# Routing, value placing and residual moved between VectorE, ScalarE, TensorE and GpSimd in an eight-part transformer kernel

## The chip, the cores and the metric

The kernel runs on one core of one Trainium2 chip. The metric is the device time of one execution, in microseconds; times below count from the start of the profiled span. The engines are TensorE (PE; PEld is its weight load), VectorE (DVE), ScalarE (ACT), GpSimd (POOL) and SyncE (SP). They run side by side, each in the order of its own list, and wait for each other on semaphores.

## The reference

Sixty-four batches of 128 tokens with 128 features go through four layers, each a cross attention and a feed-forward part, each added to its input after a layer norm. The change touches the last layer, and at its end the output:

```python
x = x + _L3_xattn_ref(_layernorm(x), ctx, ctx, Uq, Vq, bq, ... Uo, Vo, bo)
x = x + _L3_ffn_ref(_layernorm(x), router_w, w1, w2)
```

The attention of layer 3 has 16 heads of 8 features, 77 keys a batch, projections of the form `x U V + b`, and keeps the 64 largest of the 77 scores before its softmax. Its feed-forward part is a mixture of 64 experts: every token goes to the four experts with the largest router probability (position within an expert by token order, 128 places an expert), each expert computes `silu(h1) * h2` and a second product, and a token's result is the sum of its four experts' rows weighted by their probabilities.

## The kernel before, in words

All eight parts are one program. `X` (128 x 64 x 128) stays in SBUF for its whole length. `attention_layer` (from L128) writes all four attention parts; for layer 3 it is called with `topk=64`, `lowrank=True`, a context and a router. It first opens a short block: SP loads the weights (`load`, L233), the products `U V` are folded into `Wq, Wk, Wv, Wo` on TensorE (L298) and copied (L290), and `router.load` (L2426) and `router.prepare` (L2431) add what the router needs.

The main block has one list of steps for each engine, written out by `run_written_out`: step s works on several batches at once. For layer 3 (`lag = 2`) TensorE computes in step s the scores of batch s, turns the scores of batch s-2, weighs the values of s-2, turns back s-3, projects the output of s-4 (`project_out`, L439), and prepares s+1. ScalarE evacuates PSUM: `copy_scores` (L565) copies raw scores, first and second half, `probabilities` (L538, L540) makes exponentials, `copy_q` (L548) and `spread_k` (L554) fill the operands of the next scores. VectorE does the selection of the 64 largest: for each of 16 heads eight smallest distances are found (`select_eight`, L727), replaced (L735), found again (L743) and replaced (L756); between them stand `residual` (L783, adds the projected output in PSUM to `X`), `subtract_max` (L696), `norm_heads` (L676, L681), `place_v` (L774, puts the projected values with their bias into `vaug`) and `statistics` (L788). GpSimd computes `distances` (L630) and adds the output bias to `X` (`add_bias`, L618).

The router rides on the same steps, four batches (a group, 16 in all) at a time, four steps a group: on GpSimd `deviations`, `probabilities` (L2594), `chosen` (L2601, L2608: the mask of chosen experts and running counts), `place` (L2613 to L2629: the row of each token in its expert's table), `fill_rows` (L2635 to L2637) and `scatter` (L2645), 16 indirect DMAs a group that send the token rows to DRAM. On VectorE stand `minima` (L2685), `sums` (L2689), `reciprocals`, `best` (L2701), `marks` (L2715) and `keys_in_order` (L2725); on ScalarE and TensorE normalisation, logits, and positions (`copy_positions`, L2515). Group g is handled from step 4g+8 on, so its last steps lie up to 14 steps behind the last attention batch: a tail in which the routing runs alone.

Then a small block loads `own` and `rank` and clears `hid` (L2824 to L2829), the expert block runs 32 pairs of experts and sends their rows on to a table of shares, and the last block adds up: for each batch SP loads the four shares of every token (L3003, 256 KB), TensorE adds in PSUM the product of the last expert rows (L3013) and `X` through an identity product (L3015), VectorE adds the shares pairwise (L3023, L3035) and then PSUM (L3031), and ScalarE's queue stores 64 KB. Four buffers stand behind each of these tiles.

Of the kernel before, what the change touches and what calls it, by code (L numbers as in the profile page):

```python
# [127 lines left out]
def attention_layer(nc, m, k, w, heads, keys, scale, context=None, mask=None, topk=0, lowrank=False,  # L128
# [28 lines left out]
    with ExitStack() as ctx:  # L157
# [30 lines left out]
        if lowrank:  # L188
            U = sb("U", [D, 4, D])
            V = sb("V", [D, 4, D])  # L190
# [17 lines left out]
        v_ps = PS[0:keys, 7, 128:256]  # L208
# [18 lines left out]
        with nc.Block() as block:  # L227
# [3 lines left out]
            def _(sp):  # L231
# [30 lines left out]
            def _(dve):  # L262
# [24 lines left out]
                if lowrank:  # L287
                    dve.wait_ge(q["fold"], 1)
                    for n, W in enumerate((Wq, Wk, Wv, Wo)):
                        last = dve.tensor_copy(W[:, :], PS[:, 0, n * D:(n + 1) * D])  # L290
                    last.then_inc(q["prep"], 1)

            @block.tensor
            def _(pe):
                if lowrank:
# [4 lines left out]
                    last.then_inc(q["fold"], 1)  # L300
            m.weight_loads = loaded
# [26 lines left out]
        def _(pe):  # L328
# [21 lines left out]
            def project_context(i, u, h):  # L350
# [3 lines left out]
                else:  # L354
                    pe.wait_ge(q["xT"], q.nth("xT", i))
                    kv = yT
                if past(i, 1):
                    pe.wait_ge(q["v"], q.nth("v", i, 1))
                    if not topk:
                        pe.wait_ge(q[k_ready], q.nth(k_ready, i, 1))  # L360
# [4 lines left out]
                if not topk:  # L365
                    pe.matmul(kT_ps, Wk[:, :], kv[:, u, :], start=True, stop=True)
# [64 lines left out]
            def project_out(i, u):  # L431
# [3 lines left out]
                pe.wait_ge(q["v"], q.nth("v", i, -(lag + 2)))  # L435
                if router is not None:
                    router.tensor_projected(pe, i + lag + 2)
                if inner is None:
# [50 lines left out]
        def _(act):  # L489
# [67 lines left out]

            def copy_scores(i, u, half):
# [14 lines left out]
            def step(s, v, h):  # L573
# [32 lines left out]
            run_written_out(act, step, 2 if y_by_scalar else 1, max(lag + 1, beyond), slots=slots)  # L606
# [60 lines left out]
        def _(dve):  # L667
# [124 lines left out]
            def step(s, v, h):  # L792
                u, a = v % 2, (v + 1) % 2
                end, fin = s - lag - 1, s - lag - 2
                if topk:
# [3 lines left out]
                    if real(fin):  # L799
                        residual(fin, (v - lag - 2) % 2)  # L800
# [10 lines left out]
                    if real(s + 1):  # L811
                        place_v(s + 1, (v + 1) % slots)
# [1557 lines left out]
def make_router(nc, m, t, ctx, wfT, row):  # L2370
# [41 lines left out]

    def have(i):
# [8 lines left out]
    def load(sp):  # L2422
        loads = [(gate[:, :], t[n + "router_w"]), (before_f[:, :], t["c_before"]),
                 (slot0[:, :], t["c_slot0"]), (code[:, :], t["c_token"])]
# [5 lines left out]
    def prepare(dve):  # L2430
        dve.memset(ones[:, :], 1.0)  # L2431
# [159 lines left out]
    def probabilities(pool, i):  # L2591
        prob = rows_of(i)[:, :, D:D + E]
        pool.wait_ge(q["rec"], i + 1)
        pool.tensor_tensor(prob, prob, bcast(rec[:, :], 2, E), ALU.mult).then_inc(q["prob"], 1)  # L2594

    def chosen(pool, i):
        u = i % 2
        pool.wait_ge(q["marked"], i + 1)
        if i >= 1:
            pool.wait_ge(q["pos"], i)  # L2600
        pool.tensor_scalar(by_expert(mask[:, u, :]), mark[:, :].rearrange("p (g e) -> p g e", e=E + PAD)[:, :, 0:E], -1.5,  # L2601
                           None, ALU.is_lt).then_inc(q["mask"], 1)
        pool.wait_ge(q["mask"], i + 1)
        for g in range(G):
            if g or i:
                pool.wait_ge(q["ahead"], G * i + g)
            out = ahead[:, u, g + 1, :] if g < G - 1 else ahead[:, (u + 1) % 2, 0, :]
            pool.tensor_tensor(out, ahead[:, u, g, :], mask[:, u, g * E:(g + 1) * E], ALU.add).then_inc(q["ahead"], 1)  # L2608

    def place(pool, i):  # L2610
        u = i % 2
        pool.wait_ge(q["posc"], i + 1)
        pool.tensor_scalar(near[:, :], posc[:, :], CAP - 1.0, None, ALU.min).then_inc(q["near"], 1)  # L2613
        pool.tensor_scalar(over[:, :], posc[:, :], float(CAP), float(SLOTS), ALU.is_ge, ALU.mult).then_inc(q["over"], 1)
        pool.wait_ge(q["near"], i + 1)
        pool.tensor_tensor(by_expert(key[:, :]), by_expert(near[:, :]), bcast(slot0[:, :], 1, G), ALU.add) \
            .then_inc(q["key"], 1)
        pool.wait_ge(q["over"], i + 1)
        pool.tensor_tensor(far[:, :], over[:, :], mask[:, u, :], ALU.mult).then_inc(q["far"], 1)
        pool.wait_ge(q["key"], i + 1)  # L2620
        pool.tensor_tensor(near[:, :], key[:, :], mask[:, u, :], ALU.mult).then_inc(q["kept"], 1)
        if i >= 1:
            pool.wait_ge(q["skeytop"], i)
        pool.wait_ge(q["far"], i + 1)
        pool.wait_ge(q["kept"], i + 1)
        pool.tensor_tensor(skey[:, :], near[:, :], far[:, :], ALU.add).then_inc(q["skey"], 1)
        if i >= 1:
            pool.wait_ge(q["wfTps"], i)
        pool.tensor_tensor(by_expert(wf[:, :]), by_expert(far[:, :]), rows_of(i)[:, :, D:D + E], ALU.mult) \  # L2629
            .then_inc(q["wf"], 1)  # L2630

    def fill_rows(pool, i):
        pool.wait_ge(q["skeytop"], i + 1)
        s3 = skeytop[:, :].rearrange("p (g e) -> p g e", e=8)[:, :, 0:K]
        pool.tensor_copy(rows_of(i)[:, :, KEYS:KEYS + K], s3)  # L2635
        pool.tensor_copy(rows_of(i)[:, :, CODE:CODE + 1], code[:, G * i:G * i + G].unsqueeze(2))
# [600 lines left out]
```

## Time and profile before

| | |
|---|---|
| median of three runs | 3944.61 us (3942.61 to 3950.3) |
| the profiled execution's own time | 3949.06 us |
| its span | 3947.3 us |
| mean granted TensorE clock | 0.837 |
| busy: TensorE, VectorE, ScalarE, GpSimd | 76%, 76%, 57%, 48% |
| attention of layer 3 (2702 to 3634 us) | 932 us |
| routing tail (3634 to 3742 us) | 108 us |
| last block (3850.5 to 3947.3 us) | 96.8 us |

The page gives for each engine its busy time as a share of the span, and its digits cut the span into 40 slices of 98.7 us. TensorE's two clock levels are 1.2 and 2.4 GHz; a granted clock of 0.50 is the lower one. In a timeline row the first number is the start, the second the duration; xN merges neighbours of one line. The shares are averages over stages with different limits, so they are read by stage.

### The profile page before, as it was taken

What the parts mean: (1) busy time and instruction counts of PE and PEld (TensorE: products, weight loads), DVE (VectorE), ACT (ScalarE), POOL (GpSimd) and SP (SyncE); (2) the same over time, 40 slices, a digit from 0 to 9 for tenths busy, and PEclk for the clock granted to TensorE, in tenths of its full rate; (3) what the DMA queues carried; (4) which work ended last, traced back from release to release, by engine and by line L of the source; (5) the groups of instructions that cost most, each with busy time, mean ns of one, the idle gap of its engine ahead of it and who ended that gap; (6) DMA issues with size and microseconds to landing.
All of it is one profiled execution on the core that took longest, in us unless ns stands there. A gap on an engine that the chain in (4) does not pass through costs nothing. (4 is left out here: it accounts for less than half of the span.)

```text
span 3947.3 us, 77991 instructions
## 1 busy us (share of the span) xinstructions
PE 3004.5 (76%) x23435; PEld 1888.8 (48%) x23435; DVE 3014.5 (76%) x12267; ACT 2240.8 (57%) x4368; POOL 1905.5 (48%) x2166
## 2 busy tenths in 40 slices
PE   3777776999979997797599968885777767777069
PEld 1222222444447776443467745554555555555046
DVE  6999997666667776344788858887999999998065
ACT  4999997333346665242366646664666666665030
POOL 5777776000014566575444442222256666666660
PEclk9999998999989999898799979996555665655585
DMA  2000000940000010253200000000011100000037
GB/s 74 5 5 5 5 6 22 418 193 0 0 16 17 27 29 26 79 140 111 61 15 15 15 8 2 2 2 13 20 36 38 38 18 5 5 5 2 1 111 213
DMA packets 161015, 177.77 MB, mean 45 GB/s; under 512 B 71762, under 2 KB 136180, under 8 KB 153179
## 3 DMA queue, kind: packets, MB, share of 16 engines
q1 hardware_dynamic: 127964, 140.65, 11.7%
q0 software_dynamic: 23424, 27.94, 2.1%
q10 hardware_dynamic: 9216, 4.20, 0.4%
q8 instruction: 197, 3.23, 0.3%
q14 instruction: 214, 1.75, 0.1%
HBM read 80.48 MB, written 113.61 MB: 49 GB/s over the span
## 5 line engine op out<-in xcount | busy, mean ns | idle before, releaser
L395 PE MATMUL PS<-IDENT,a_T 128*77 128x128 f32 (+1 forms) x3584 | 618.3, 313 | 132.0 <-ACT a_Pr L540 110.5
L1037 ACT ACTIVATE l_H<-l_H 128x2048 f32<-128x2048 f32 (+2 forms) x256 | 597.3, 2702 | 2.8 <-POOL l_H L1089 2.6
L395 PEld LDWEIGHTS PS<-IDENT,a_T 128*77 128x77 f32 (+1 forms) x3584 | 487.0, 171 | 226.8 <-ACT a_Pr L540 88.6
L1089 POOL TENSOR_TENSOR l_H<-l_feat,l_text 128x4096 f32<-128x4096 f32 x64 | 450.4, 7039 | 131.5 <-PE PS L993 130.8
L993 PE MATMUL PS<-l_H,l_wide 128*32 128x512 f32 (+1 forms) x2560 | 332.2, 595 | 165.3 <-ACT l_H L1037 165.3
L1111 DVE TENSOR_TENSOR l_H<-PS,l_text 128x2048 f32<-128x2048 f32 (+1 forms) x192 | 411.7, 2146 | 2.1 <-ACT l_text L1064 2.1
L542 ACT ACTIVATE a_Pr<-PS 77x512 f32<-77x512 f32 (+1 forms) x640 | 375.4, 588 | 59.4 <-PE PS L395 59.4
L412 PE MATMUL PS<-a_Pr,a_vaug 77*32 77x128 f32 (+1 forms) x7168 | 303.9, 316 | 21.8 <-ACT a_OT L571 15.8
L630 POOL TENSOR_TENSOR a_T<-a_mx,a_T 128x616 f32<-128x616 f32 x128 | 155.5, 1215 | 307.4 <-DVE a_mx L696 307.4
L2645 POOL DMA_INDIRECT expert_rows<-e3r_row,e3r_rows_at x256 | 253.6, 991 | 86.7 <-issue 73.6
L109 POOL TENSOR_TENSOR RSTD<-norm_tmp,MINUS_HALF 128x24 f32<-128x24 f32 x6 | 25.1, 4189 | 553.3 <-DVE norm_tmp L102 553.3
L338 PE MATMUL PS<-a_kblk,a_qT 32*128 32x308 f32 (+1 forms) x2048 | 243.1, 549 | 24.2 <-ACT e3r_posc L2515 7.4
L637 POOL TENSOR_TENSOR a_T<-a_T,a_mx 128x616 f32<-128x616 f32 x128 | 155.6, 1216 | 204.0 <-DVE a_mx L712 204.0
L412 PEld LDWEIGHTS PS<-a_Pr,a_vaug 77*32 77x32 f32 (+1 forms) x7168 | 214.1, 125 | 76.2 <-issue 54.2
L528 ACT ACTIVATE a_yT<-PS 128x128 f32<-128x128 f32 x192 | 53.3, 278 | 301.1 <-PE PS L348 301.1
L993 PEld LDWEIGHTS PS<-l_H,l_wide 128*32 128x32 f32 x2560 | 57.5, 109 | 342.7 <-ACT l_H L1037 294.6
L735 DVE MATCH_REPLACE8 a_T<-a_r,a_T 128x77 f32<-128x77 f32 x1024 | 213.6, 222 | 0.3 <-issue 0.3
L756 DVE MATCH_REPLACE8 a_T<-a_r,a_T 128x77 f32<-128x77 f32 x1024 | 213.6, 223 | 0.0
L429 PE MATMUL PS<-IDENT,a_O 128*128 128x128 f32 x256 | 86.1, 336 | 160.0 <-DVE a_O L681 160.0
L714 DVE TENSOR_REDUCE a_mx<-PS 128x8 f32<-128x616 f32 (+1 forms) x256 | 189.2, 739 | 22.9 <-PE PS L338 13.7
L1492 ACT ACTIVATE e_act_g<-PS 128x512 f32<-128x512 f32 x128 | 76.5, 597 | 225.8 <-PE PS L1444 225.6
L716 DVE TENSOR_TENSOR a_T<-PS,a_mx 128x616 f32<-128x616 f32 (+1 forms) x256 | 190.8, 745 | 8.8
(356 smaller groups left out, 7857.7 us busy)
## 6 DMA issues: line engine op xcount, KB each, us to landing
pair_rows<-e_zero SPq DMA_DIRECT2D x35, 1024.0 KB, 25.3
expert_shares<-e_zero SPq DMA_DIRECT2D x16, 1024.0 KB, 25.7
e3c_four<-expert_shares SPq DMA_DIRECT2D x64, 256.0 KB, 3.2
e_xin<-pair_rows SPq DMA_DIRECT2D x39, 264.0 KB, 3.2
e_four<-pair_shares SPq DMA_DIRECT2D x16, 512.0 KB, 4.5
e_w<-in_L_ffn_blocks SPq DMA_DIRECT2D x39, 194.0 KB
e3x_xin<-expert_rows SPq DMA_DIRECT2D x32, 200.0 KB
expert_rows<-e_zero SPq DMA_DIRECT2D x6, 1024.0 KB, 24.8
```

What stands on the lines that cost most here:

```text
L338: last = pe.matmul(PS[:, g, 0:hpg * keys], qT[32 * g:32 * g + 32, u, :], kblk[32 * g:32 * g + 32, u, :], start=True, stop=True, tile_posit ...
L395: last = pe.transpose(PS[0:keys, 4 + g % 2, j * S:(j + 1) * S], T[:, u, c:c + keys], m.IDENT[:, :])
L412: last = pe.matmul(PS[32 * j:32 * j + 32, 6, g * S:(g + 1) * S], vaug[:, v, c * 32:c * 32 + 32], Pr[:, u, c * S:(c + 1) * S], start=(p == ...
L542: act.activation(part, turned, ACT.Exp).then_inc(q[f"P{g}"], 1)
L716: dve.tensor_tensor(t4, raw, bcast(m4, 3, keys), ALU.subtract).then_inc(q[f"sfree{half}"], 1)
L735: last = dve.match_replace(t3[:, h, :], r1[:, u, 8 * h:8 * h + 8], t3[:, h, :], FAR)
L756: last = dve.match_replace(t3[:, h, :], r2[:, u, 8 * h:8 * h + 8], t3[:, h, :], FAR)
L993: last = pe.matmul(PS[32 * j:32 * j + 32, 4 + u, 0:cols], wide[:, 32 - r:64 - r], H[:, u, CH * c * S:CH * c * S + cols], start=(r == 0), s ...
L1037: act.activation(cells, cells, ACT.Tanh).then_inc(q[f"tanh{part}"], 1)
L1089: pool.tensor_tensor(H[:, a, lo * S:hi * S].rearrange("p (t f) -> p t f", f=S), bcast(feat[:, a, :], 1, hi - lo), bcast(text[:, a, lo:hi], ...
L1111: dve.tensor_tensor(H[:, u, lo * S:hi * S].rearrange("p (t f) -> p t f", f=S), bcast(PS[:, 1 + u, 0:S], 1, hi - lo), bcast(text[:, u, lo:h ...
L2645: pool.indirect_dma_start(out=m.rows[:, :], out_offset=bass.IndirectOffsetOnAxis(ap=rows_at[:, i % 3, g * K + k:g * K + k + 1], axis=0), i ...
```

## The change

- **Values.** `place_v` of VectorE is replaced by `place_v_plain` on ScalarE, a copy of the projected values from PSUM without their bias. The bias of the values is instead carried through the output projection once, in the setup: `bv` as a column is widened to a 128 x 128 tile, multiplied by `Wo`, and added to `bo`. The projected values move from bank 7 to bank 4 and are computed together with keys and queries.
- **Residual.** In `project_out` an identity product adds `X` (with the output bias already in it) in PSUM, and ScalarE writes the sum to `X` (`write_x`). `residual` leaves VectorE's list for this layer.
- **Late routing.** `probabilities` of group 15, `chosen` of groups 14 and 15, `place` and `fill_rows` of groups 13 to 15 are issued by VectorE instead of GpSimd.
- **Setup of the experts.** `own`, `rank` and `hid` are loaded and cleared in the attention layer's setup; the block of their own goes.
- **Last block.** For odd batches TensorE's identity product goes; VectorE adds `X` to the half sum, waits for that, and goes on.

```diff
@@ setup of the lowrank layer @@
+                if lowrank:
+                    load(bv_col[:, :], w.bv.unsqueeze(1))
...
-                    last.then_inc(q["prep"], 1)
+                    dve.tensor_copy(bv_wide[:, :], bv_col[:, 0:1].broadcast_to([D, S])).then_inc(q["prep"], 1)
+                    dve.wait_ge(q["fold"], 2)
+                    dve.tensor_tensor(bo[:, :], bo[:, :], PS[:, 1, 0:D], ALU.add)
...
+                    pe.wait_ge(q["prep"], m.preps + 3)
+                    pe.matmul(PS[:, 1, 0:D], bv_wide[:, :], Wo[:, :], start=True, stop=True).then_inc(q["fold"], 1)
@@ TensorE @@
                 if topk:
                     pe.matmul(kT_ps, Wk[:, :], cT[:, u, :], start=True, stop=True)
+                    pe.matmul(v_ps, cT[:, u, :], Wv[:, :], start=True, stop=True)
...
+                        pe.wait_ge(q["v"], q.nth("v", i, -lag))
...
+                if topk:
+                    if past(i, 1):
+                        pe.wait_ge(q["x"], q.nth("x", i, 1))
+                    pe.matmul(out_ps, OT[:, u, :], Wo[:, :], start=True, stop=False)
+                    pe.wait_ge(q["bias"], q.nth("bias", i))
+                    last = pe.matmul(out_ps, m.IDENT[:, :], seq(m.X, i), start=False, stop=True)
@@ ScalarE @@
+            def place_v_plain(i, v):
+                if past(i, slots):
+                    act.wait_ge(q["pv"], q.nth("pv", i, slots))
+                act.activation(head_columns(vaug[:, v, :], hps)[:, :, :, 0:dh],
+                               v_ps.rearrange("p (t a e) -> p t a e", a=hps, e=dh), ACT.Copy).then_inc(q["v"], 1)
+
+            def write_x(i):
+                act.wait_ge(q["out"], q.nth("out", i))
+                act.activation(seq(m.X, i), out_ps, ACT.Copy).then_inc(q["x"], 1)
...
                     probabilities(use, (v - lag) % 2, 0)
+                if topk and real(use - 2):
+                    write_x(use - 2)
...
                         spread_k(s + 1, a)
+                        place_v_plain(s + 1, (v + 1) % slots)
@@ VectorE @@
-                    if real(fin):
-                        residual(fin, (v - lag - 2) % 2)
...
-                    if real(s + 1):
-                        place_v(s + 1, (v + 1) % slots)
@@ router @@
+    late_weighed, late_chosen, late_placed = NG - 1, NG - 2, NG - 3
...
+        if v == 0 and have(c - 3) and c - 3 >= late_weighed:
+            probabilities(dve, c - 3)
+        if v == 2 and have(c - 3) and c - 3 >= late_placed:
+            place(dve, c - 3)
...
+        if v == 0 and have(c - 3) and c - 3 >= late_chosen:
+            chosen(dve, c - 3)
+        if v == 2 and have(c - 3) and c - 3 >= late_placed:
+            fill_rows(dve, c - 3)
@@ last block @@
-                    pe.matmul(PS[:, s % 4, 0:D], m.IDENT[:, :], m.X[:, s, :], start=False, stop=True) \
-                        .then_inc(q["far"], 1)
+                    if s % 2 == 0:
+                        last = pe.matmul(PS[:, s % 4, 0:D], m.IDENT[:, :], m.X[:, s, :], start=False, stop=True)
+                    last.then_inc(q["far"], 1)
...
+                        if w % 2:
+                            dve.tensor_tensor(two[:, w, 0:D], two[:, w, 0:D], m.X[:, s - 1, :], ALU.add) \
+                                .then_inc(withx, 1)
+                            dve.wait_ge(withx, (s - 1) // 2 + 1)
```

## Rows read from the trace of the kernel before

**Rows 1.** Windows by stage: window, length, each engine's busy us, PEclk, DMA share, GB/s.

```profile
2702.00:3634.00 932.00, 675.55 (x4672) 496.27 (x4672) 911.18 (x6892) 592.13 (x1376) 538.26 (x770) 0.58 0.06 18
3634.00:3742.00 108.00, 19.10 (x129) 14.40 (x128) 12.32 (x86) 13.08 (x33) 82.74 (x114) 0.50 0.02 1
3850.50:3947.30 96.80, 92.69 (x256) 63.87 (x256) 52.92 (x192) 0.00 (x0) 0.00 (x0) 0.50 0.76 217
```

**Rows 2.** Timeline of VectorE from L727 to what follows: start, us, line, operation.

```profile
2727.55 0.22 DVE L727 MAX8 a_r<-a_T 128x8 f32<-128x77 f32 x1
2727.91 0.09 DVE L735 MATCH_VALUE_LOAD a_T<-a_r,a_T 128x8 f32 x1
...
2766.38 2.33 DVE L727 MAX8 a_r<-a_T 128x8 f32<-128x77 f32 x16
2768.62 0.27 DVE L783 TENSOR_TENSOR X<-PS,X 128x128 f32<-128x128 f32 x1
2768.85 0.09 DVE L735 MATCH_VALUE_LOAD a_T<-a_r,a_T 128x8 f32 x1
...
3260.55 0.27 DVE L783 TENSOR_TENSOR X<-PS,X 128x128 f32<-128x128 f32 x1
3260.74 0.41 DVE L2685 TENSOR_REDUCE e3r_mn<-e3r_nl 128x4 f32<-128x256 f32 x1
```

**Rows 3.** Timeline of VectorE at L774.

```profile
3267.83 0.27 DVE L774 TENSOR_TENSOR a_vaug<-PS,a_bv 77x128 f32<-77x128 f32 x1
3268.01 0.41 DVE L2689 TENSOR_REDUCE e3r_lsum<-e3r_row 128x4 f32<-128x256 f32 x1
```

**Rows 4.** Timelines of TensorE, ScalarE, VectorE in the step with least margin.

```profile
3243.60 1.41 PE L338 MATMUL PS<-a_kblk,a_qT 32*128 32x308 f32 x8 [0.53 <-ACT e3r_posc L2515]
...
3247.89 0.66 ACT L565 ACTIVATE a_T<-PS 128x616 f32<-128x616 f32 x1
...
3249.68 0.78 DVE L696 TENSOR_REDUCE a_mx<-a_T 128x8 f32<-128x616 f32 x1
```

**Rows 5.** Timeline of the setup block, SP's last issues.

```profile
2696.30 0.43 SPq L2426 DMA_DIRECT2D e3r_slot<-in_c_slot  x1
2696.77 0.43 SPq L2426 DMA_DIRECT2D e3r_code<-in_c_token  x1
```

**Rows 6.** Timeline of the small block ahead of the experts, SP.

```profile
3749.47 0.33 SPq L2824 DMA_DIRECT2D e3x_own<-in_c_own  x1
...
3752.00 12.15 SPq L2840 DMA_DIRECT2D e3x_xin<-expert_rows  x6
```

**Rows 7.** Timelines of the routing tail, GpSimd, and one row of ScalarE.

```profile
3645.76 0.38 ACT L2515 ACTIVATE e3r_posc<-PS 128x256 f32<-128x256 f32 x1
...
3653.83 1.09 POOL L2645 DMA_INDIRECT expert_rows<-e3r_row,e3r_rows_at  x1 [0.79 <-POOL e3r_rows_at L2637]
...
3680.93 0.97 POOL L2645 DMA_INDIRECT expert_rows<-e3r_row,e3r_rows_at  x1 [0.31 <-issue]
...
3689.04 1.09 POOL L2645 DMA_INDIRECT expert_rows<-e3r_row,e3r_rows_at  x1 [0.79 <-POOL e3r_rows_at L2637]
...
3698.10 0.97 POOL L2645 DMA_INDIRECT expert_rows<-e3r_row,e3r_rows_at  x1 [0.30 <-issue]
...
3701.77 0.86 POOL L2601 TENSOR_SCALAR e3r_mask<-e3r_mark 128x256 bf16<-128x256 f32 x1 [2.06 <-DVE e3r_mark L2715]
...
3704.58 1.07 POOL L2645 DMA_INDIRECT expert_rows<-e3r_row,e3r_rows_at  x1 [0.41 <-issue]
```

**Rows 8.** Last block: one window, VectorE's first and thirteenth L3023, landing of the stores.

```profile
3866.00:3874.00 8.00, 8.00 (x23) 5.53 (x23) 4.74 (x16) 0.00 (x0) 0.00 (x0) 0.50 0.98 294
...
3853.35 0.42 DVE L3023 TENSOR_TENSOR e3c_two<-e3c_four 128x256 f32<-128x256 f32 x1 [15.48 <-DMA e3c_four<-expert_shares]
...
3866.17 0.42 DVE L3023 TENSOR_TENSOR e3c_two<-e3c_four 128x256 f32<-128x256 f32 x1 [0.20 <-DMA e3c_four<-expert_shares]
...
DMA to landing us min/median/max: 1.5/2.9/5.3
```

More of the change, by code:

```diff
@@ L603, in step @@
                         spread_k(s + 1, a)
+                        place_v_plain(s + 1, (v + 1) % slots)
                 if router is not None:
                     router.scalar_end(act, s)
-            run_written_out(act, step, 2 if y_by_scalar else 1, max(lag + 1, beyond), slots=slots)
+            run_written_out(act, step, 2 if y_by_scalar else 1, max(lag + 2, beyond), slots=slots)
         @block.gpsimd
@@ L2367, in clear_rows, with make_router @@
     sp.wait_ge(m.s_cleared, n)
-def make_router(nc, m, t, ctx, wfT, row):
+def make_router(nc, m, t, ctx, wfT, row, own, rank, hid):
     n = "L3_ffn_"
@@ L2423, in load @@
         loads = [(gate[:, :], t[n + "router_w"]), (before_f[:, :], t["c_before"]),
-                 (slot0[:, :], t["c_slot0"]), (code[:, :], t["c_token"])]
+                 (slot0[:, :], t["c_slot0"]), (code[:, :], t["c_token"]), (own[:, :], t["c_own"]),
+                 (rank[:, :], t["c_rank"])]
         for dst, src in loads:
@@ L2430, in prepare @@
     def prepare(dve):
+        dve.memset(hid[:, :, :], 0.0)
         dve.memset(ones[:, :], 1.0)
@@ L2604, in chosen @@
         for g in range(G):
             if g or i:
-                pool.wait_ge(q["ahead"], G * i + g)
+                eng.wait_ge(q["ahead"], G * i + g)
             out = ahead[:, u, g + 1, :] if g < G - 1 else ahead[:, (u + 1) % 2, 0, :]
-            pool.tensor_tensor(out, ahead[:, u, g, :], mask[:, u, g * E:(g + 1) * E], ALU.add).then_inc(q["ahead"], 1)
-    def place(pool, i):
+            eng.tensor_tensor(out, ahead[:, u, g, :], mask[:, u, g * E:(g + 1) * E], ALU.add).then_inc(q["ahead"], 1)
@@ L2611, in place @@
+    def place(eng, i):
         u = i % 2
[L2612 to L2616, printed above, removed]
+        eng.wait_ge(q["posc"], i + 1)
+        eng.tensor_scalar(near[:, :], posc[:, :], CAP - 1.0, None, ALU.min).then_inc(q["near"], 1)
+        eng.tensor_scalar(over[:, :], posc[:, :], float(CAP), float(SLOTS), ALU.is_ge, ALU.mult).then_inc(q["over"], 1)
+        eng.wait_ge(q["near"], i + 1)
+        eng.tensor_tensor(by_expert(key[:, :]), by_expert(near[:, :]), bcast(slot0[:, :], 1, G), ALU.add) \
@@ L2617, in place @@
             .then_inc(q["key"], 1)
[L2618 to L2621, printed above, removed]
+        eng.wait_ge(q["over"], i + 1)
+        eng.tensor_tensor(far[:, :], over[:, :], mask[:, u, :], ALU.mult).then_inc(q["far"], 1)
+        eng.wait_ge(q["key"], i + 1)
+        eng.tensor_tensor(near[:, :], key[:, :], mask[:, u, :], ALU.mult).then_inc(q["kept"], 1)
@@ L2622, in place @@
         if i >= 1:
[L2623 to L2626, printed above, removed]
+            eng.wait_ge(q["skeytop"], i)
+        eng.wait_ge(q["far"], i + 1)
+        eng.wait_ge(q["kept"], i + 1)
+        eng.tensor_tensor(skey[:, :], near[:, :], far[:, :], ALU.add).then_inc(q["skey"], 1)
         if i >= 1:
-            pool.wait_ge(q["wfTps"], i)
@@ L2657, in pool_first @@
             pads(pool, c - 2)
-        if v == 2 and have(c - 3):
+        if v == 2 and have(c - 3) and c - 3 < late_placed:
             place(pool, c - 3)
@@ L2780, in layer3 @@
         lastT = sb("last", [2 * E, D])
+        own, rank = sb("own", [CAP, E]), sb("rank", [CAP, K])
+        hid = sb("hid", [CAP, 2, 4 * I])
         q = Signals(ctx, nc, "e3", [
-            "consts", "coded", "meta", "in0", "in1", "in2", "in3", "xT", "xTs",
+            "coded", "meta", "in0", "in1", "in2", "in3", "xT", "xTs",
             "up", "gate", "hid", "hidT", "hidTs", "down", "rank", "ress", "held", "sent0", "sent1", "sent2", "sent3",
@@ L2789, in layer3 @@
             row = inner.enter_context(nc.sbuf_tensor("e3r_row", [S, 3, G * ROW], F32))
-            router = make_router(nc, m, t, inner, wfT, row)
+            router = make_router(nc, m, t, inner, wfT, row, own, rank, hid)
             def weights(sp, i):
@@ L2806, in sc @@
                 return inner.enter_context(nc.sbuf_tensor(f"e3x_{name}", shape, dt))
-            own, rank = sc("own", [CAP, E]), sc("rank", [CAP, K])
             xin = sc("xin", [CAP, 4, 2 * ROW])
@@ L2819, in layer3 @@
             stage = sc("stage", [CAP, NP, 2 * D])
-            with nc.Block() as block:
-                @block.sync
-                def _(sp):
-                    sp.dma_start(own[:, :], t["c_own"]).then_inc(q["consts"], 16)
-                    sp.dma_start(rank[:, :], t["c_rank"]).then_inc(q["consts"], 16)
-                @block.vector
-                def _(dve):
-                    dve.memset(hid[:, :, :], 0.0)
-                    dve.wait_ge(q["consts"], 32)
             block = inner.enter_context(nc.Block())
```

56 lines of the change are left out of this document (29 added, 27 removed).

## The prediction

> **What bounds the kernel now.** I read the busy digits of the page first: the changed code lies in the last third of the span, so I cut that third into stages with the windows view [rows 1]. Three of them are touched. From 2702 to 3634 us the lowrank attention layer runs: VectorE is busy 911 of 932 us, ScalarE 592, TensorE 676, GpSimd 538. That is a stage bound by VectorE's instruction stream; nothing else is near it. From 3634 to 3742 us only GpSimd works without pause: it sends the last routed rows, with routing arithmetic between the sends. From 3850.5 us to the end TensorE is busy 92.7 of 96.8 us on 128 products (two records each). So each of the three edits takes work from the engine that bounds its stage, and the question of each is what is late next.
>
> **Attention, VectorE loses two adds a batch.** The adds are `residual` (L783) and `place_v` (L774). A busy time of 0.27 us each would suggest 0.54 us a batch, but their starts and their neighbours' starts say less [rows 2, 3]. The instruction behind L774 starts 0.18 us after it (3267.83 to 3268.01; 0.19 in nearly all the others). Nothing behind it waits for L743's result until much later, so its removal gives 0.19 us. The first two attention batches place their values outside the stream; 62 are on the path: 62 x 0.19 = 11.8 us. L783 stands between L727 and L735, and L735 must wait for L727's last result. In the steps before the first residual the gap from L727's end to L735 is 0.14 us (2727.55 + 0.22 to 2727.91); with L783 in it, it is 0.14 us too (2766.38 + 2.33 to 2768.85). The add is hidden in a wait that stays: removing it gives nothing in those steps. Only where the router's L2685 stands behind it (one step in four, 14 times) does everything move up by 0.19 us (3260.55 to 3260.74): 2.7 us. **Together 14.5 us**; the upper bound is 33.5 (62 x 0.27 x 2), the lower one follows below.
>
> The Trainium skill, VectorE: DVE Perf Modes, section "The DRAIN you can't avoid", says that the next operation does not start until the pipe has emptied and that one should cut the number of operations, not semaphores; by it the sum would hold the 33.5. The rows above disagree: starts are 0.19 apart under a busy time of 0.27, and one of the two adds stands in a gap that is there without it.
>
> **Attention, what is added.** ScalarE gets two copies out of PSUM a batch, of 128 columns each; the router's copy of 256 columns takes 0.38 us [rows 7], so at most 49 us come to 592 busy of 932 [rows 1]. TensorE gets one identity product a batch; at the pace of the last stage (92.7 / 128) that is 0.72 us, 46 us on 676. Neither is the bound by share. What counts is the chain from scores to ScalarE's first copy (L565) to VectorE's maximum (L696), which the new pieces lengthen by at most 0.72 (product) + 0.38 (`write_x` ahead of that copy) + 0.38 (`place_v_plain` at the end of ScalarE's step) = 1.48 us. I compared the end of each first copy with the start of its maximum: the tightest kind is one step in four, 3247.89 + 0.66 to 3249.68, 1.13 us [rows 4]. In that step TensorE already idles 0.53 us before the scores for a router copy, which takes up part of the product. So at most 0.95 us of the 1.13 is spent, and VectorE arrives 0.19 sooner: the cover is just used up, cost nothing. Without the 0.53 it would be 0.54 us in 16 steps, 9 us, which makes 6 us the lower bound of the stage's gain. The new waits: TensorE's product waits for `bias` (made by GpSimd four steps before) and for the previous `x` (written by ScalarE in the step before, well ahead); behind it the scores are queued. `write_x` waits for a product that TensorE issues ahead of the transposes for which ScalarE waits anyway. `statistics` waits for ScalarE half a step later. Values now lie in bank 4, so the transposes wait for `v`, which ScalarE writes 3 us or more earlier. All nothing.
>
> **Setup.** Three more loads stand in SP's list (bv column, own, rank) at the pitch of its issues, 0.47 us [rows 5], and the products wait for the last: +1.4 us. The new fold (copy, product, add) follows the last weight copy serially: 0.27 + 0.72 + 0.28 = +1.3 us. The memset of `hid` lies under the products. In return the little block ahead of the experts goes: from its first load at 3749.47 to the experts' first at 3752.00, -2.5 us [rows 6]. **Net +0.2 us**, bounds -1 and +2.
>
> **Tail, GpSimd loses the routing of the last groups.** Its sends run at 0.97 + 0.31 = 1.28 us each. Between send starts that hold routing, the surplus over 1.28 is what goes [rows 7]: `place` and `fill_rows` of group 14, 3680.93 to 3689.04, 6.8 us, and the same again for group 15; `probabilities` and `chosen` of group 15, 3698.10 to 3704.58, 5.2 us; `chosen` of group 14, which is that less the 2.06 of waiting in it and 0.6 of probabilities (an estimate below L2601's 0.86 over the same columns), 2.5 us. Group 13's `place` does not vanish wholly: its positions are there at 3645.76 + 0.38, and seven VectorE operations, the heads' division, four maxima and three small copies follow; at some 0.4 us and less each I estimate 4.4 us, 3650.6, and the 0.8 us that GpSimd takes from there to a send gives 3651.4 against 3653.83: 2.4 us. Are the later groups' chains ready in time? I count forward from 3651.4: two sendings of four (10.2 us each for eight sends) and the statistics of group 15 bring GpSimd to 3696 before it needs group 15's rows, whose chain (normalise by 3668, then some 25 operations on three engines at up to 0.7 us) I estimate to end at 3685: 11 us of cover. **Sum 6.8 + 6.8 + 5.2 + 2.5 + 2.4 = 23.7 us**; bounds 21 (group 13 gives nothing) and 28 (it gives all).
>
> **The end.** Odd batches lose their identity product: TensorE's pace falls from 2 x 0.72 = 1.45 us a batch to 1.08. VectorE has 52.9 / 64 = 0.83 busy a batch and gets 0.27 (as L783) and a wait on itself of 0.1 for every other: 1.02. The transfers come next: a batch moves 256 KB in and 64 KB out, 327680 bytes. In the window where they are densest they make 294 GB/s at a share of 0.98 [rows 8], 1.115 us a batch; and from the first load's use to the thirteenth 12 batches take 12.82 us, 1.07. So TensorE, VectorE and the queues all end within 0.1 us of each other, and the slowest is taken: 2.8 (first load, 3850.5 to 3853.35) + 63 x 1.115 + 4.9 (the last store's median landing 2.9, and 2 estimated for the last sums) = 77.9 against 96.8: **-18.9 us**. Bounds: -21 at TensorE's own pace; and none at all if each store needed its longest landing, 5.3 us (four buffers: (5.3 + 0.6) / 4 = 1.47), though the median is 2.9.
>
> TensorE is granted 0.50 of its clock, 1.2 GHz, in this stage, right through windows in which it is busy 8.00 of 8.00 us [rows 8]. The Trainium skill, TensorE: Matmul & The Clock Gate, section "The HAM clock gate", says that sustained activity releases the throttle; by it the stage would run at the upper level, be bound by transfers already, and the edit there would give 0. The row disagrees.
>
> **Sum.** -14.5 + 0.2 - 23.7 - 18.9 = -56.9 us. The profiled execution took 3949.06 us (span 3947.3), which becomes 3892.2; it lies 4.4 above the median of the runs, 3944.61, and from that the forecast is 3887.7 us, say 3888.
>
> **Rivals.** (a) The end turns on jitter of the stores: a store lands after 1.5 to 5.3 us [rows 8], and with three engines within 0.1 us of each other stalls no longer hide. At a pace of 1.27 the gain there is 9: 3897.5 us. For it, the landing times; against, the 1.07 over 12 batches was reached with the stores running. Chance 0.2. (b) VectorE gets the full busy time of both adds back, 33.5: 3869 us. Against it the two gaps of 0.14. Chance 0.06. (c) A late group's chain gates GpSimd for 10 us (VectorE works strictly in order, so `place` of group 13 holds the last batch's division and, through it, group 15's statistics): 3898 us. Against it the 11 us of cover. Chance 0.08. (d) The clock of the last stage was up to chance and rises: transfers bind, 0 to 19 lost of the gain; 3888 to 3907. Chance 0.04. (e) Slower than before: the longer chain through TensorE and ScalarE becomes the attention layer's bound. Taking the tight step's 1.13 us for the margin of all 64, a chain longer by d loses 64 x (d - 1.13), which eats 57 us from d = 2.0 us on; I count 0.95 to 1.48. At d = 2.1 it gives 3950 us. Chance 0.03. (f) The edits do not act (compiled to the same waits, or covered by the layer's fixed ends): 3944. Chance 0.02. The forecast keeps 0.57.
>
> **Chances and range.** A difference of 0.2%, about 8 us, is what a measurement of this kernel can tell from no change. All cases but (e) and (f) are faster by more: 0.95 faster, 0.02 same, 0.03 slower. The range goes from (b), 3868, to just short of the end giving nothing, 3905.
>
> **What the next profile would show.** In the attention stage: no L774 and L783 on VectorE, a period shorter by 0.19 us in three steps of four and by 0.38 in the fourth, VectorE still busy over 97%, and L696 never waiting for L565. If it waits, (e) has begun. In the tail: sends of 1.28 us without gaps from about 3637 on except before group 13's. In the end stage: about 78 us, DMA share over 0.93, TensorE no longer without gaps. The prediction is wrong where the end stage stays over 85 us, or the attention stage shrinks by other than 12 to 18 us.

## The result and the profile after

The changed kernel takes 3888.11 us (median, 3880.54 to 3890.78) against 3947.45 us of the kernel before in the same comparison: ratio 0.9852, 95% interval 0.984 to 0.9864, or 59 us less (the medians as they stand; the ratio makes it 58). Its profiled execution took 3887.59 us with a span of 3885.8; before these were 3949.06 and 3947.3. Windows by stage of the changed kernel (window, length, busy us of PE, PEld, DVE, ACT, POOL, then PEclk, DMA share, GB/s), to be held against [rows 1]. Each kernel has its own line numbers: in the changed one the first maxima are L756, the first replacement L764, the second maxima L772, the last replacement L785 (before: L727, L735, L743, L756), ScalarE's copy of the scores is L591, VectorE's maximum of them L725, the sends are L2676, and the first addition of the last block is L3053.

```profile
2702.50:3619.50 917.00, 660.04 (x4795) 491.08 (x4796) 889.19 (x6766) 611.54 (x1501) 538.09 (x770) 0.64 0.06 18
3619.50:3704.00 84.50, 19.21 (x135) 14.64 (x133) 22.19 (x124) 13.55 (x36) 60.46 (x73) 0.52 0.02 1
3704.00:3711.20 7.20, 0.00 (x0) 0.00 (x0) 0.00 (x0) 0.00 (x0) 0.00 (x0) 0.50 0.00 0
3711.20:3809.70 98.50, 62.64 (x384) 48.36 (x384) 62.96 (x320) 34.89 (x98) 62.20 (x64) 0.86 0.38 111
3809.70:3885.80 76.10, 65.34 (x192) 45.98 (x192) 59.41 (x224) 0.00 (x0) 0.00 (x0) 0.50 0.89 277
```

The attention layer has gone from 932 to 917 us, the routing tail from 108 to 84.5, the last block from 96.8 to 76.1. TensorE is no longer busy all through the last block, at the same granted clock of 0.50. Measured between the same instructions in both traces:

| part of the sum | predicted | traces |
|---|---|---|
| attention, 64 steps of the first selection | -14.5 | -14.6 |
| setup ahead of it | +2.7 | +2.4 |
| tail, first send after group 13's `chosen` to last send | -23.7 | -23.7 (104.34 to 80.60) |
| small block ahead of the experts | -2.5 | -2.6 |
| experts' block | 0 | 0 (98.5 in both) |
| last block | -18.9 | -20.7 |

The rest of the 61.5 us between the two spans, 1.9 us, lies ahead of the setup, in code that is the same in both.

VectorE at the gap of [rows 2], without the residual and then with the router's reduction in it (the two lines of the second pair now follow each other directly):

```profile
2768.19 0.22 DVE L756 MAX8 a_r<-a_T 128x8 f32<-128x77 f32 x1
2768.56 0.09 DVE L764 MATCH_VALUE_LOAD a_T<-a_r,a_T 128x8 f32 x1
...
3252.65 0.40 DVE L2716 TENSOR_REDUCE e3r_mn<-e3r_nl 128x4 f32<-128x256 f32 x1
3252.97 0.08 DVE L764 MATCH_VALUE_LOAD a_T<-a_r,a_T 128x8 f32 x1
```

The replacement still starts 0.15 us after the last maximum ends (2768.41 to 2768.56), as it did with the residual in between. GpSimd and VectorE where group 13 is sent, to be held against [rows 7]:

```profile
3622.18 1.13 POOL L2676 DMA_INDIRECT expert_rows<-e3r_row,e3r_rows_at  x1 [0.43 <-issue]
...
3631.26 0.97 POOL L2676 DMA_INDIRECT expert_rows<-e3r_row,e3r_rows_at  x1 [0.30 <-issue]
3636.65 0.97 POOL L2676 DMA_INDIRECT expert_rows<-e3r_row,e3r_rows_at  x1 [4.42 <-DVE e3r_rows_at L2668]
...
3702.78 0.97 POOL L2676 DMA_INDIRECT expert_rows<-e3r_row,e3r_rows_at  x1 [0.31 <-issue]
```

From 3640 us on the sends follow at 1.28 us; what else GpSimd does there is group 14's probabilities and group 15's statistics (3648.2 to 3652), which the change leaves to it. Group 15's rows are known long before they are needed:

```profile
3669.46 0.17 DVE L2668 TENSOR_SCALAR e3r_rows_at<-e3r_skeytop 128x16 uint32<-128x16 f32 x1
```

Its first send is due at 3702.78 - 15 x 1.28 = 3683.6. In the last block the chain of what ended last has changed hands; before it was 90% TensorE's two products, now (chain by line, share of the block):

```profile
by line: DMA e3c_four<-expert_shares 49.4%; DMA out<-e3c_done 12.1%; DVE e3c_done L3061 8.9%; issue 7.1%; DVE e3c_sums L3069 6.8%; DVE e3c_two L3053 6.4%; DVE e3c_two L3066 3.0%; DVEq L3060 0.1%
```

### The profile page after: what moved, and what is told of

It is laid out like the page before. It is cut to its first block and busy times, and to the rows that moved or that the text cites. A ratio compares the mean times of both kernels' runs of the same rounds, so it can differ in the third digit from the quotient of the medians.

```text
span 3885.8 us, 78038 instructions
## 1 busy us (share of the span) xinstructions
PE 2962.6 (76%) x23501; PEld 1869.2 (48%) x23501; DVE 3009.3 (77%) x12214; ACT 2259.2 (58%) x4496; POOL 1882.8 (48%) x2125
## 5 line engine op out<-in xcount | busy, mean ns | idle before, releaser
L405 PE MATMUL PS<-IDENT,a_T 128*77 128x128 f32 (+1 forms) x3584 | 588.3, 302 | 157.9 <-ACT a_Pr L556 138.6
L405 PEld LDWEIGHTS PS<-IDENT,a_T 128*77 128x77 f32 (+1 forms) x3584 | 464.2, 164 | 243.3 <-ACT a_Pr L556 105.5
L2676 POOL DMA_INDIRECT expert_rows<-e3r_row,e3r_rows_at x256 | 253.5, 990 | 89.4 <-issue 74.7
L346 PE MATMUL PS<-a_kblk,a_qT 32*128 32x308 f32 (+1 forms) x2048 | 239.8, 543 | 14.8 <-ACT a_kblk L570 5.8
L544 ACT ACTIVATE a_yT<-PS 128x128 f32<-128x128 f32 x192 | 53.2, 277 | 304.8 <-PE PS L356 304.8
L785 DVE MATCH_REPLACE8 a_T<-a_r,a_T 128x77 f32<-128x77 f32 x1024 | 213.7, 223 | 0.5 <-issue 0.5
L764 DVE MATCH_REPLACE8 a_T<-a_r,a_T 128x77 f32<-128x77 f32 x1024 | 213.7, 223 | 0.0
L743 DVE TENSOR_REDUCE a_mx<-PS 128x8 f32<-128x616 f32 (+1 forms) x256 | 189.1, 739 | 22.5 <-PE PS L346 13.2
```

The source lines that it names most:

```text
L346: last = pe.matmul(PS[:, g, 0:hpg * keys], qT[32 * g:32 * g + 32, u, :], kblk[32 * g:32 * g + 32, u, :], start=True, stop=True, tile_posit ...
L405: last = pe.transpose(PS[0:keys, 4 + g % 2, j * S:(j + 1) * S], T[:, u, c:c + keys], m.IDENT[:, :])
L764: last = dve.match_replace(t3[:, h, :], r1[:, u, 8 * h:8 * h + 8], t3[:, h, :], FAR)
L785: last = dve.match_replace(t3[:, h, :], r2[:, u, 8 * h:8 * h + 8], t3[:, h, :], FAR)
L2676: pool.indirect_dma_start(out=m.rows[:, :], out_offset=bass.IndirectOffsetOnAxis(ap=rows_at[:, i % 3, g * K + k:g * K + k + 1], axis=0), i ...
```

## Experiments

### One part of the change at a time

Four kernels take the kernel before and one part of the change each; the kernel before took 3947.44 us beside them, against 3947.45 beside the changed kernel, and I count the two as one chip, "the first", on the strength of that. `last_only` has the last hunk of the diff alone, `late_only` the router's.

> The kernel before with the edit of the last block alone (odd batches' X added by VectorE). Theory (TensorE at the lower clock binds the block, transfers come next): the prediction's step gives -18.9 us; the two traces show the block going from 96.8 to 76.1 us, so -20.7 us if the edit acts alone, ratio 0.9948. TensorE stays at 1.2 GHz. Rival (the clock would have risen, or transfers bound the block already): 0 us, ratio 1.000. Rival (stores' jitter, a pace of 1.27 us a batch): -9 to -11 us, ratio 0.9975.

Measured: 3925.37 against 3947.44 us, ratio 0.995 (0.9937 to 0.9964), -20 us by the ratio (the medians lie 22 apart). Its last block takes 78.3 us of 96.8, which is 18.5 less; the same code took 76.1 in the changed kernel, so the block's length itself varies by some 2 us from program to program:

```profile
3844.30:3922.60 78.30, 65.00 (x192) 45.95 (x192) 59.44 (x224) 0.00 (x0) 0.00 (x0) 0.50 0.87 269
```

The clock stayed at 1.2 GHz, and the attention layer was as before (913.2 us between the first and last starts of the second selection, 913.0 before). Both rivals that make it 0 are out; -9 to -11 lies outside the interval.

> The kernel before with the late groups' routing on VectorE alone. Theory: -23.7 us, ratio 0.9940, the same sends at 1.28 us without gaps except before group 13's, and nothing on the attention layer. Rival (late chain): a send waits some 10 us for group 15, -13.7 us, ratio 0.9965. Rival (VectorE still works on attention when group 13 is placed, so that place costs the stream what GpSimd saves): up to 7 us less gain, ratio 0.9958.

Measured: 3918.18 us, ratio 0.9935 (0.9921 to 0.9948), -26 us by the ratio (the medians lie 29 apart). From the end of the attention (last start of the second selection, 3621.9) to the last send (3707.4) it takes 85.5 us, before 109.3 (3631.7 to 3741.0): -23.8. Attention again 913.1. So the routing moved to VectorE costs its stream nothing, and no send waits for group 15.

```diff
@@ residual_only: the change's project_out and write_x, values as before @@
+                    pe.matmul(out_ps, OT[:, u, :], Wo[:, :], start=True, stop=False)
+                    pe.wait_ge(q["bias"], q.nth("bias", i))
+                    last = pe.matmul(out_ps, m.IDENT[:, :], seq(m.X, i), start=False, stop=True)
...
-                    if real(fin):
-                        residual(fin, (v - lag - 2) % 2)
@@ values_only: bias fold, values in bank 4 and on ScalarE, residual as before @@
-                    if real(s + 1):
-                        place_v(s + 1, (v + 1) % slots)
...
+                        place_v_plain(s + 1, (v + 1) % slots)
```

> The kernel before with only the residual moved from VectorE to TensorE (identity product) and ScalarE. Theory (the add stands in a gap of 0.14 us that stays without it, except where the router's L2685 stands behind it): 14 x 0.19 = -2.7 us, ratio 0.9993. Rival (each add on VectorE costs its busy time): 62 x 0.27 = -16.7 us, ratio 0.9958. Rival (it costs the start-to-start 0.19 in all steps): -11.8 us, ratio 0.9970. Rival (the longer chain through TensorE and ScalarE costs something): above 1.000.

> The kernel before with only the placing of the values moved to ScalarE, their bias folded into the output's bias in the setup. Theory: 62 x 0.19 = -11.8 us in the attention layer, +1.8 us in the setup (one load 0.47, copy, product and add 1.3), together -10.0 us, ratio 0.9975. Rival (busy time): -16.7 + 1.8 = -14.9 us, ratio 0.9962. With residual_only this should make the attention layer's -14.6 us; if the two are coupled, their sum misses it.

Measured: residual_only 3944.04 us, ratio 0.9995 (0.9986 to 1.0004); values_only 3937.51 us, ratio 0.9974 (0.9965 to 0.9983). The first interval reaches from -5.5 to +1.6 us and leaves out -16.7 and -11.8; the second reaches from -13.8 to -6.7, holds the expected -10.0 and leaves out -14.9. The traces say it by step. The table gives the time between starts of `statistics` on VectorE, in each of the four steps of a group once the router runs (typical of 10 or more, they repeat to 0.02 us), and the stage from first to last start of the second selection:

| us | step A | step B | step C | step D | stage |
|---|---|---|---|---|---|
| before | 14.77 | 14.46 | 14.54 | 14.54 | 913.0 |
| residual_only | 14.77 | 14.46 | 14.35 | 14.54 | 909.8 |
| values_only | 14.59 | 14.26 | 14.35 | 14.35 | 902.2 |
| after | 14.59 | 14.26 | 14.15 | 14.35 | 898.1 |

Taking the residual off VectorE changes nothing in three steps and 0.19 us in the fourth (C, which holds the reduction [rows 2]); the value placing is worth 0.19 in all four. The gap is there in residual_only as before:

```profile
3224.71 2.33 DVE L739 MAX8 a_r<-a_T 128x8 f32<-128x77 f32 x16
3227.19 0.09 DVE L747 MATCH_VALUE_LOAD a_T<-a_r,a_T 128x8 f32 x1
```

The parts add up. By the ratios the four kernels are 0.50, 0.65, 0.05 and 0.26% faster, together 1.46% for the 1.48% of the whole change. By stage it is 18.5 + 23.8 + 3.2 + 10.8 = 56.3 us for 58 to 59, and the missing 2 us are those by which the last block is shorter in the changed kernel than in last_only; setup and small block cancel.

### What the gap is, and what it is worth

If the 0.15 us are the wait of L764 for L756's own last result, they go when nothing stands right behind what it waits for. The same pattern stands at the small memset ahead of the last replacements (L780, then L785 0.24 us later in 62 of the changed kernel's 64 batches):

```profile
2762.51 0.10 DVE L780 MEMSET a_r<- 128x48 f32 x1
2762.76 0.09 DVE L785 MATCH_VALUE_LOAD a_T<-a_r,a_T 128x8 f32 x1
```

```diff
@@ split_wait @@
+                    if h == heads // 2 - 1:
+                        last.then_inc(q["r1half"], 1)
                 last.then_inc(q["r1"], 1)
...
-                dve.wait_ge(q["r1"], q.nth("r1", i))
+                dve.wait_ge(q["r1half"], q.nth("r1half", i))
                 pass_wait()
                 for h in range(heads):
+                    if h == heads // 2:
+                        dve.wait_ge(q["r1"], q.nth("r1", i))
+                        pass_wait()
@@ early_cut @@
+                    if real(s - 1):
+                        cut_rest(s - 1, a)
                     if real(s):
                         subtract_max(s, u, h, 1)
```

> The changed kernel, in which the first eight replacements wait only for the first eight of the sixteen maxima just found (the last eight for all), so that nothing stands right behind the result that it waits for. Theory (the gap of 0.14 us between the last MAX8 and the first replacement is the wait for the engine's own last result, and the next instruction would otherwise start 0.08 before that MAX8's end): 0.22 us less in the 48 batches whose gap is empty, nothing in those with the router's reduction in it, -10.6 us, ratio 0.9825 against the kernel before (0.9852 for the changed kernel). Rival (the gap is the price of going from one kind of instruction to another): 0.9852.

> The changed kernel with the small memset ahead of the last replacements moved ahead of the second maximum, so that its waiter no longer stands right behind it. Theory: 0.24 us between the memset's start and the first replacement's becomes the memset's own pitch of at most 0.10: 64 x 0.15 = -9.6 us, ratio 0.9828. Rival (no gain, the engine empties itself before any replacement): 0.9852.

> Both edits: -20.2 us against the changed kernel, about 3868 us, ratio 0.9801, VectorE busy without a gap in the attention steps. Rival (once VectorE is faster by 0.37 us a batch the chain through TensorE and ScalarE, with its least margin of 0.85 us, becomes the bound): less, with VectorE waiting at its maximum for ScalarE's copy; ratio 0.983.

These three, and all runs after them, ran on two other chips, where the whole program is slower: the kernel before takes 4077 us beside these three and 4059 to 4073 beside the later ones, most of it outside the stages told of here. Ratios: split_wait 0.9866 (0.9833 to 0.9899), early_cut 0.9843 (0.9812 to 0.9874), both_gaps 0.9833 (0.9805 to 0.9861). The intervals are too wide to tell the three from 0.9852, so the steps are read:

| us | step A | step B | step C | step D | stage |
|---|---|---|---|---|---|
| after's attention code, first chip | 14.59 | 14.26 | 14.15 | 14.35 | 898.1 |
| the same on another chip (no_x, below) | 14.59 | 14.5 to 14.8 | 14.2 to 15.2 | 14.35 | 910.4 |
| split_wait | 14.34 | 14.7 to 15.2 | 14.2 to 15.3 | 14.10 | 904.9 |
| early_cut | 14.31 | 14.6 to 14.8 | 14.1 to 15.4 | 14.05 | 901.2 |
| both_gaps | 14.06 | 14.6 to 14.9 | 13.9 to 15.4 | 13.80 | 896.5 |

In steps A and D the wait split saves 0.25 us (expected 0.22), the earlier memset 0.28 to 0.30 (expected 0.15; it starts only 0.02 us ahead of the maximum), both together 0.53 to 0.55. The steps ahead of the router's show the same: 13.75 us becomes 13.50, 13.47 and 13.23. In split_wait the replacement starts 0.08 us before the last maximum ends (3012.85), and in both_gaps the memset is followed at once:

```profile
3010.52 2.33 DVE L756 MAX8 a_r<-a_T 128x8 f32<-128x77 f32 x16
3012.77 0.08 DVE L769 MATCH_VALUE_LOAD a_T<-a_r,a_T 128x8 f32 x1
```

```profile
2853.12 0.10 DVE L783 MEMSET a_r<- 128x48 f32 x1
2853.14 0.75 DVE L725 TENSOR_REDUCE a_mx<-a_T 128x8 f32<-128x616 f32 x1
2853.80 0.08 DVE L791 MATCH_VALUE_LOAD a_T<-a_r,a_T 128x8 f32 x1
```

So the gap is the wait, not a price of changing the kind of instruction. Each such place costs 0.25 us a step, more than taking an add away (0.19). But of 62 x 0.54 = 33 us only 13.9 arrive (910.4 - 896.5), because steps B and C do not follow: both_gaps' rival, the chain through TensorE and ScalarE, holds them.

### Why two steps of four do not follow

> The changed kernel with ScalarE's first copy of the scores made two more times ahead of the one that counts (0.71 us each, so the chain to VectorE's maximum is 1.42 us longer and ScalarE 91 us busier). From the margins of the changed kernel's 64 batches (least 0.85, typical 1.4 to 4.3 us) the theory expects VectorE to wait in about 5 batches, 1 to 3 us in all. Rival (the new pieces had used the cover up, as the prediction counted for the tightest kind): 16 x 1.3 = 20 us more if the tightest kind has none left, 80 us if no batch has.

> The same with four more copies, 2.84 us. Theory, as the sum of what goes beyond each batch's margin: 32 us more than the changed kernel, VectorE waiting in some 38 batches, total about 3920 us. Rival (delays are made up again by later steps' margins): clearly less than 32. Rival (cover used up): 100 us and more.

```diff
@@ copy_scores, chain2 (chain4: four) @@
+                if half == 0:
+                    for k in range(2):
+                        act.activation(t4, PS[:, banks, 0:hpg * keys], ACT.Copy).then_inc(q["again"], 1)
+                        act.wait_ge(q["again"], 2 * i + k + 1)
```

Measured: chain2 4056.23 us, ratio 0.9994 (0.9976 to 1.0012), chain4 4132.74 us, 1.0184 (1.0136 to 1.0231). Stages 954.2 and 1029.3 us, 44 and 119 more than no_x's 910.4: far above the 1 to 3 and 32 that I had from the first chip's margins. VectorE's waits in the attention layer, of chain2 and of the same code without the longer chain (waiter, awaited: us in total, times, longest):

```profile
DVE a_mx L729 <- ACT a_T L595: 39.5, 37, 1.8
DVE e3r_lsum L2724 <- ACT e3r_row L2561: 10.7, 13, 0.9
```

```profile
DVE e3r_lsum L2720 <- ACT e3r_row L2557: 6.3, 8, 0.9
DVE a_mx L725 <- ACT a_T L591: 2.3, 8, 0.4
```

The second pair, from no_x, shows that on this chip VectorE waits for ScalarE already in the changed kernel. On the first chip the changed kernel's stage shows none from 2760 us on. What is late is one copy of ScalarE. In the first chip's trace L544 starts 0.04 us after the product that it copies (L356) has ended, in all 64 batches; in no_x it comes 1.3 to 2.9 us late in 12 batches, one in four from the 20th on, and is punctual within 0.15 us in the others:

```profile
3323.89 0.39 ACT L512 ACTIVATE a_oT<-PS 128x256 f32<-128x256 f32 x1
3328.33 0.28 ACT L544 ACTIVATE a_yT<-PS 128x128 f32<-128x128 f32 x1 [4.05 <-remote]
3328.51 0.58 ACT L554 ACTIVATE a_Pr<-PS 77x512 f32<-77x512 f32 x1
...
3329.66 0.26 ACT L582 ACTIVATE X<-PS 128x128 f32<-128x128 f32 x1
3329.90 0.68 ACT L591 ACTIVATE a_T<-PS 128x616 f32<-128x616 f32 x1
...
3330.61 0.80 DVE L725 TENSOR_REDUCE a_mx<-a_T 128x8 f32<-128x616 f32 x1 [0.41 <-ACT a_T L591]
```

TensorE's product was done at 3325.43. The tight step kind, whose margin was 1.35 to 2.4 us on the first chip, then has none. With the margins of this chip (0 in B and C, 1.15 in D) chain2 should cost 1.42 x 24 + 0.27 x 12 = 37 us plus what the router's sum adds; it cost 44, with steps B at 16.1, C at 16.6, D at 14.72. So the law of margins held, and its numbers did not carry from one chip to the other.

Why L544 comes late is open. It needs nothing but that product and one long past, and the profile names a remote release. Loads of instructions lie near some of the late copies but not others, and near punctual ones too. Such late copies, up to 3.1 us, stand in all eight traces from the other two chips (11 or 12 of more than 0.4 us in each; five in chain4, whose copies come later by its own chain), and in none of the six from the first: there all 64 start after 0.04 us, in the kernel before as in the changed one. The kernel before has no trace on the other chips.

The last kernel closes both gaps and takes 0.16 us off the chain:

> Both gaps closed as in both_gaps, and ScalarE's write of X issued behind its first copy of the scores instead of ahead of it (0.16 us off the chain to VectorE's maximum). From the periods of both_gaps in the steps where VectorE waits for nobody (14.06 and 13.80 us against 14.59 and 14.35 of the changed kernel) closing both gaps is worth 0.53 to 0.55 us a step. Theory A, on a chip where ScalarE's yT copy (L544) starts right behind TensorE's product in every step: 62 x 0.54 = -33 us against the changed kernel less a few us of waiting in the two tight kinds of step, ratio 0.977 to 0.980 against the kernel before, the attention stage (first to last L772 group start) 865 to 875 us against 898. Theory B, on a chip where that copy comes 2 to 3 us late once in four steps, as in both_gaps: the stage some 893 us (both_gaps 896.7), because two kinds of step gain 0.53 and the two others are held by ScalarE; ratio about 0.982.

Measured: 4007.51 against 4072.94 us, ratio 0.9847 (0.9822 to 0.9871), stage 896.8 us, as both_gaps' 896.5; steps A and D 14.06 and 13.81, B 14.6, C mostly 15.5. Neither theory A nor B's 893: the 0.16 us is gained in B and lost in C, where VectorE then waits for the router's row. No version clearly beats the changed kernel where it was measured. What closing the gaps brings on a chip without the late copy was not tried; from steps A and D I estimate at most 33 us.

### What binds the last block now

> The changed kernel with no X added in the last block at all (the output lacks its last residual). TensorE then needs 0.72 us a batch and VectorE 0.83. Theory (transfers bind the block now): the pace stays within 0.05 of 1.067 us a batch, the block 73 to 76 us against 76.1. Rival (TensorE at 1.085 or VectorE at 1.02 still bind): the pace falls towards 0.83, the block to some 62 us.

> The changed kernel with X added by VectorE in every batch of the last block. TensorE needs 0.72 us a batch; VectorE 1.06 a batch (an odd batch of the changed kernel, 3823.36 to 3824.42). Theory: transfers at 1.067 and VectorE at 1.06 side by side, stalls of the stores no longer made up: 76 to 80 us for the block. Rival (TensorE bound the changed kernel's block): it becomes shorter than 76.1.

```diff
@@ no_x (all_x_vector: the add for every batch instead) @@
-                    if s % 2 == 0:
-                        last = pe.matmul(PS[:, s % 4, 0:D], m.IDENT[:, :], m.X[:, s, :], start=False, stop=True)
...
-                        if w % 2:
-                            dve.tensor_tensor(two[:, w, 0:D], two[:, w, 0:D], m.X[:, s - 1, :], ALU.add) \
-                                .then_inc(withx, 1)
-                            dve.wait_ge(withx, (s - 1) // 2 + 1)
```

Measured (one run each, 4010.25 and 4017.04 us; no_x leaves out the last residual, so its output is not the reference's): the block takes 76.6 us without any X and 78.7 with all of it on VectorE. The changed kernel's own code takes 76.1 (and 78.3 in last_only) on the first chip, 77.2 to 78.8 in the three kernels of the gaps, and 77.8 to 79.6 in chain2, late_write and chain4, on the chip of these two. Windows of no_x's and all_x_vector's last block:

```profile
3931.90:4008.50 76.60, 47.73 (x128) 30.86 (x128) 51.35 (x192) 0.00 (x0) 0.00 (x0) 0.50 0.88 275
```

```profile
3936.60:4015.30 78.70, 48.72 (x128) 30.78 (x128) 67.08 (x256) 0.00 (x0) 0.00 (x0) 0.50 0.86 267
```

TensorE loses a quarter of its work (65.3 to 47.7 us), VectorE an eighth, and no_x's block is 1 to 3 us shorter than those of the changed code on the same chip, which is no more than equal code differs by (76.1 to 79.6) and far from the rival's 62: transfers bind the block, and moving X further buys little. A load also has to wait until one of four buffers is free, and SyncE waits for VectorE's release 60 times in the changed kernel and in no_x alike. Whether the bytes or these four buffers set the transfers' pace was not tried; the DMA share, 0.92 to 1.03 in the changed kernel's 8 us windows between 3818 and 3880 us, speaks for the bytes.

## Why the prediction was right

**What bounds each stage** held: three stages, three engines, and each gain came within 2 us of what its own rows gave. That 3888 was met to the microsecond is luck: the median of the kernel before was 2.8 us higher in the comparison than the one I had started from, and the gain 2.4 us larger.

**The two adds.** The count by starts, 0.19 us, and the claim that the residual's add lies in a wait that stays, were the step with most at stake (14.5 against 33.5 us). residual_only and values_only confirm it by step. I had called the gap a wait for the engine's own result on the strength of two rows; split_wait shows it. I did not see what follows from it: that the wait itself, at 0.25 us, was worth more than the add. The Trainium skill, VectorE: DVE Perf Modes, section "The DRAIN you can't avoid", says that a semaphore after each operation costs nothing extra, which it measured on eight tensor_copy. In steps A and D of split_wait, moving one such wait away from right behind its operation saves 0.25 us, so here it does cost. The prediction also drew too much from that section: the same section says that a next operation that is not held starts earlier, which the 0.19 us between starts bears out, so the 33.5 does not follow from it.

**The chain of TensorE and ScalarE.** Nothing was lost on the chip of the profile, as forecast, but the size was wrong. I counted 0.95 us of a margin of 1.13 as spent. In the trace after, the tight kind has 1.35 to 2.4 us, and 0.85 in one step. `write_x` delays its neighbour by 0.16 us, not 0.38; behind the value copy ScalarE idles in 43 of 64 batches; the identity product ends 0.43 us behind the product before it in 59 of 64 batches, where I had 0.72:

```profile
3239.12 0.25 ACT L582 ACTIVATE X<-PS 128x128 f32<-128x128 f32 x1
3239.28 0.67 ACT L591 ACTIVATE a_T<-PS 128x616 f32<-128x616 f32 x1
```

```profile
3234.68 0.78 PE L451 MATMUL PS<-a_Wo,a_OT 128*128 128x128 f32 x2
3235.24 0.63 PE L453 MATMUL PS<-X,IDENT 128*128 128x128 f32 x2
```

I had taken durations here and starts for VectorE, in the same text. Rival (e) was priced for a longer chain of the kernel's own. What came on the other chips is its mild form from another cause: 12.3 us more in the attention layer (910.4 against 898.1), so that the gain there should be nearer 47 than 59 us, if the kernel before loses nothing to late copies there, which no trace shows. The changed kernel itself was not run there; the two with its attention layer lie 49 and 42 us under the kernel before (4010.25 and 4017.04 against 4059.4), one run each. For the six others I estimate its gain from each ratio and from what that kernel's attention stage differs from 910.4: 44 to 55 us. So the forecast came true for the chip whose trace it was made from, and is some 2 to 15 us too good for the other two.

**Setup, small block, tail.** +2.4 for +2.7, -2.6 for -2.5, -23.7 for -23.7. Group 13's wait was seen rightly: GpSimd stands 4.42 us for `rows_at`. Group 15's chain was over-estimated: it ends 14 us before the need, where I had 11. Rival (c) is out.

**The last block** came out 1.8 us better than forecast in the changed kernel (76.1 for 77.9) and 0.4 worse in last_only (78.3), with the same code. I took 1.115 us a batch from the densest 8 us of before; VectorE's first additions now start 1.067 us apart (3812.49 to 3879.73, 63 batches), the pace of the first 12 batches before, which I had named but not used, and 1.102 apart in last_only. So the pace was right within 5%, and which of the two values a run shows is open. What 1.115 rested on was no limit: in windows of 8 us the transfers now reach 320 GB/s, above the 294 of a block that TensorE was still holding back:

```profile
3828.00:3836.00 8.00, 8.00 (x26) 5.57 (x24) 7.10 (x28) 0.00 (x0) 0.00 (x0) 0.50 1.03 320
```

Rival (a), jitter of the stores, is out: VectorE waits for a store three times, 1.8 us in all, though their median landing rose from 2.9 to 3.6 us. Rival (d) is out: the clock is 0.50 in every window of the block.

## What to carry to other kernels

Price an operation that leaves a saturated in-order engine by the distance of starts around it, and look whether its neighbour waits for a result just made: if so the operation was free, and the wait is the thing to remove, by putting any other instruction between producer and waiter. Price what is added to the helping engines the same way, against the least margin in each kind of step, and do not trust a margin of 1 or 2 us from one chip's trace.

## What the runs showed that I had not expected

- A wait for an instruction's own engine placed right behind its producer costs 0.25 us on VectorE (steps A and D of split_wait), 0.28 to 0.30 behind a memset of 48 columns.
- On two chips other than the first, one ScalarE copy in four steps starts up to 3 us after everything the profile shows it to need; the cause is open.
- A block that one engine holds back understates what its transfers can do: in windows of 8 us 294 GB/s at best before, 320 in one after.
- The last block took 76.1 us in the changed kernel and 78.3 in last_only, with the same code and the same time of the kernel before beside both; a difference of 2 us in such a stage needs more than one trace.
